# Rests split by time between GpSimd and VectorE, one division for all heads, and no fc1 product of block 1 among the heads of block 0

## The reference

```python
# block 0: int8-like activations, ternary weights, 16 heads of 32 columns
xn = rmsnorm(x, g1) * (1 + scale) + shift
q, k, v = split_heads(bitlinear(xn, w_qkv, b_qkv))
attn = softmax(q @ k.T * 32 ** -0.5)            # per head
o = merge_heads(attn @ v)
x = x + bitlinear(o, w_proj, b_proj)            # act_quant takes max |o| of each row
xn = rmsnorm(x, g2) * (1 + scale2) + shift2
x = x + bitlinear(gelu(bitlinear(xn, w_fc1, b_fc1)), w_fc2, b_fc2)
# block 1: float32, one head of 512 columns
h = film(rmsnorm(x))
x = x + softmax(Q(h) @ K(h).T * 512 ** -0.5) @ V(h) @ proj_w + proj_b
h = film2(rmsnorm(x))
return x + gelu(h @ mlp_w1 + mlp_b1) @ mlp_w2 + mlp_b2
```

## Time and profile before

| | us |
|---|---|
| median of 3 runs | 2530.7 |
| lowest and highest run | 2521.5 and 2537.11 |
| the profiled execution, its time | 2516.55 |
| its span, first to last instruction | 2514.7 |
| mean granted TensorE clock, share of full | 0.923 |
| ScalarE busy, share of the span | 1225.0, 49% |
| GpSimd busy, share of the span | 768.5, 31% |

### The profile page before, as it was taken

How to read it: one execution, slowest core, us unless ns; L and a number is a source line. 1 busy time by engine, 2 the same in 40 slices (tenths; PEclk the granted TensorE clock), 3 DMA queues, 4 the chain that set the end, 5 groups by cost and what they waited for, 6 DMA issues and landing times.

```text
span 2514.7 us, 40181 instructions
## 1 busy us (share of the span) xinstructions
PE 2120.9 (84%) x13525; PEld 1069.9 (43%) x13525; DVE 1683.9 (67%) x2870; ACT 1225.0 (49%) x2032; POOL 768.5 (31%) x684
## 2 busy tenths in 40 slices
PE   4667688878997799779997899789988898789989
PEld 3424344444444444344444444344444344444434
DVE  4578645877578666877578756967587757866422
ACT  6535334474436554464446544564447444574330
POOL 0135101353125422353125412343136312452112
PEclk8777888989999899989999899989999899999989
DMA  7554111302230122202230213102231213101202
GB/s 276 192 181 164 59 51 34 94 18 76 78 113 22 52 75 96 83 18 76 85 105 22 76 51 121 58 29 82 85 97 31 71 60 124 34 35 51 101 23 95
DMA packets 85507, 200.82 MB, mean 80 GB/s; under 512 B 7604, under 2 KB 48856, under 8 KB 73120
## 3 DMA queue, kind: packets, MB, share of 16 engines
q1 hardware_dynamic: 77512, 174.91, 20.6%
q10 hardware_dynamic: 7776, 23.07, 2.6%
HBM read 161.97 MB, written 35.72 MB: 79 GB/s over the span
## 4 chain that ended last, share of the span: by engine, by line
PE 55%; DVE 17%; issue 13%; ACT 10%; POOL 2%; DMA 2%; ACTq 1%; DVEq 0%; SPq 0%; POOLq 0%
PE banks L1213 10%; PE banks L1214 10%; PE banks L1215 10%; PE banks L1170 5%; PE banks L1105 5%; DVE memory L997 4%; PE banks L1061 4%; DVE memory L1046 2%; ACT memory L1042 2%; DVE memory L814 2%; PE banks L991 2%; PE banks L900 1%; ACT L1042 1%; ACT memory L847 1%; PE banks L1035 1%
## 5 line engine op out<-in xcount | busy, mean ns | idle before, releaser
L1213 PE MATMUL banks<-memory 128*128 128x512 bf16 x1536 | 599.8, 390 | 46.9 <-DVE memory L1463 26.6
L1214 PE MATMUL banks<-memory 128*128 128x512 bf16 x1536 | 597.3, 389 | 0.0
L1215 PE MATMUL banks<-memory 128*128 128x512 bf16 x1536 | 595.3, 388 | 0.0
L1046 POOL TENSOR_TENSOR memory<-memory 128x512 bf16<-128x512 f32 x320 | 356.3, 1125 | 499.2 <-ACT memory L1042 497.4
L1042 ACT ACTIVATE memory<-banks 128x512 f32<-128x512 f32 x512 | 283.9, 597 | 216.7 <-PE banks L1035 179.8
L997 DVE TENSOR_REDUCE memory<-banks 128x1 f32<-128x512 f32 x512 | 330.2, 679 | 52.0 <-PE banks L991 51.0
L1441 POOL TENSOR_TENSOR memory<-memory 128x512 bf16<-128x512 f32 x128 | 163.2, 1275 | 512.5 <-DVE memory L1436 512.5
L991 PE MATMUL banks<-memory 96*128 96x512 bf16 x512 | 197.2, 415 | 103.8 <-DVE memory L997 94.4
L1213 PEld LDWEIGHTS banks<-memory 128*128 128x128 bf16 x1536 | 153.6, 100 | 242.0 <-DVE memory L1463 35.0
L1061 PE MATMUL banks<-memory 128*128 128x66 bf16 x4096 | 177.7, 209 | 76.6 <-DVE memory L1046 67.0
L1215 PEld LDWEIGHTS banks<-memory 128*128 128x128 bf16 x1536 | 153.6, 100 | 192.3 <-issue 19.2
(11 more groups left out here) (169 smaller groups left out, 3115.9 us busy)
## 6 DMA issues: line engine op xcount, KB each, us to landing
memory<-weight_parts SPq DMA_DIRECT2D x80, 1024.0 KB, 4.9
memory<-head_parts SPq DMA_DIRECT2D x192, 128.0 KB, 2.7
head_parts<-memory SPq DMA_DIRECT2D x64, 256.0 KB, 2.2
weight_parts<-memory ACTq DMA_DIRECT2D x10, 1024.0 KB, 5.0
memory<-in_L_cond_w_fc SPq DMA_DIRECT2D x2, 4096.0 KB, 14.3
memory<-in_x SPq DMA_DIRECT2D x32, 256.0 KB, 3.2
memory<-ada_rows SPq DMA_DIRECT2D x16, 512.0 KB, 4.6
memory<-in_L_cond_mlp_w ACTq DMA_DIRECT2D x8, 1024.0 KB, 8.8
```

Of the source, the lines that this page charges most:

```text
L1046: eng.tensor_tensor(prob_lo[:, e % RING], expo[:, e % RING], prob_hi[:, e % RING], ALU.subtract).then_inc(ok.sem, 1)
L1213: pe.matmul(bank, lh, rh, start=(k == 0), stop=False)
L1214: pe.matmul(bank, lh, rl, start=False, stop=False)
L1215: mm = pe.matmul(bank, ll, rh, start=False, stop=(k == KC - 1))
```

## The change

- `prob_low`: exponentials 0 to 40 have their rest taken on GpSimd, 41 to 63 on VectorE (FIRST_DVE).
- A head is no longer divided by itself. ScalarE copies its high result out of bank 4 into y (`copy_head`, one slot after the weighing, COPY_AT), VectorE takes the reciprocal of the sums and adds the low result in place. After the last head VectorE divides all of y in four instructions (`divide0`), one for each row tile, before the row maxima.
- M_AT is empty: all products of M come after the slots. Products 0 and 1 stand between head 14 and head 15 on TensorE.
- The tables move: heads are weighed with lags (6, 7, 7, 7) in place of (8, 6, 6, 7); the film turns go from (2, 4) to (2, 10) to (2, 7) to (2, 13); maxima and late q/k parts move by one to three slots.
- GpSimd's four x1 biases follow products 0 to 3 instead of 6 to 9.

```diff
-LATE_HIGH = {(0, 5): ("q", 2), (0, 9): ("k", 2), (1, 4): ("q", 3), (1, 8): ("k", 3)}
-LATE_LOW = {(0, 7): ("q", 2), (0, 11): ("k", 2), (1, 5): ("q", 3), (1, 9): ("k", 3)}
-VALUE_LAG, READ_LAG = ((8, 6, 6, 7), 1)
+LATE_HIGH = {(0, 5): ('q', 2), (0, 9): ('k', 2), (1, 4): ('q', 3), (1, 9): ('k', 3)}
+LATE_LOW = {(0, 6): ('q', 2), (0, 12): ('k', 2), (1, 5): ('q', 3), (1, 9): ('k', 3)}
+VALUE_LAG, COPY_LAG, READ_LAG = ((6, 7, 7, 7), 1, 1)
+FIRST_DVE = 41
+COPY_AT = {later(at, COPY_LAG): h for at, h in VALUES_AT.items()}
-M_AT = ((3, 0), (3, 4), (3, 8), (3, 12), (4, 0), (4, 6))
+M_AT = ()
-TURN_AT = ((2, 4), (2, 6), (2, 8), (2, 10))
+TURN_AT = ((2, 7), (2, 9), (2, 11), (2, 13))
-MAX_AT = {(0, 19): 0, **{(c, 10): c for c in range(1, KC)}}
+MAX_AT = {(0, 19): 0, (1, 8): 1, (2, 10): 2, (3, 10): 3}
-LOW_DVE = [e for e in range(KC * HEADS) if (e % 4 == 3 if e < 3 * HEADS else e % 4 != 0)]
+LOW_DVE = [e for e in range(KC * HEADS) if e >= FIRST_DVE]
...
+        def head_parts(h):
+            o = banks[:, 4, 0:TT * 2 * LOW].rearrange("p (t s n) -> p t s n", t=TT, s=2)
+            return o[:, :, 0, 0:HD], o[:, :, 1, 0:HD], o[:, :, 0, HD], y[:, :, h * HD:(h + 1) * HD]
+        def copy_head(act, i, h):
+            ready(act, plan0, ("o", h), i)
+            high, _, _, out = head_parts(h)
+            act.activation(out, high, ACT.Copy).then_inc(o_copied.sem, 1)
         def read_head(dve, i, h):
             b = ready(dve, plan0, ("o", h), i)
-            dve.reciprocal(sum_inv[:, h % 2], o[:, :, 0, HD]).then_inc(o_small.sem, 1)
...
-            dve.tensor_tensor(o_parts, o[:, :, :, 0:HD], r, ALU.mult).then_inc(free[b].sem, 1)
-            done(dve, plan0, ("o", h), i)
-            dve.tensor_tensor(y[:, :, h * HD:(h + 1) * HD], o_parts[:, :, 0], o_parts[:, :, 1], ALU.add
-                              ).then_inc(o_ok.sem, 1)
+            _, low, total, out = head_parts(h)
+            dve.wait_ge(o_copied.sem, o_copied(i, h + 1))
+            dve.reciprocal(sum_inv[:, :, h], total).then_inc(o_small.sem, 1)
+            dve.tensor_tensor(out, low, out, ALU.add).then_inc(free[b].sem, 1)
+        def divide0(dve, i):
+            done(dve, plan0, ("o", H - 1), i)
+            dve.wait_ge(o_small.sem, o_small(i, H))
+            for t in range(TT):
+                r = sum_inv[:, t].unsqueeze(2).to_broadcast([P, H, HD])
+                dve.tensor_tensor(by_head(y[:, t]), by_head(y[:, t]), r, ALU.mult).then_inc(o_ok.sem, 1)
...
                 for n, job in enumerate(M):
-                    if n >= M_IN:
-                        lows1(j, [job])
-                    if j is not None and M_IN <= n < M_IN + TT:
-                        residual_bias1(pool, j, 1, n - M_IN)
+                    lows1(j, [job])
+                    if j is not None and n < TT:
+                        residual_bias1(pool, j, 1, n)
...
+                if i is not None:
+                    for (c, _), h in COPY_AT.items():
+                        if c > KC:
+                            copy_head(act, i, h)
```

## The result

| | before | after |
|---|---|---|
| median, us | 2533.9 (4 runs) | 2392.84 (4 runs) |
| lowest and highest | 2521.5 and 2542.21 | 2389.83 and 2395.39 |
| the profiled execution | 2516.55 | 2395.26 |

The ratio is 0.9447, with a 95% interval from 0.9403 to 0.949. Ratios compare fast runs alone: beside the kernel without table loads and the one with everything that helped, two of seven runs of before were slow (2538.69 and 2544.43 us).

A forecast was written before the change was run, and what follows sets the result against it. It took VectorE to bound the first half of the heads and ScalarE the second. Seven items at -6.8 us (-48) and item 0 at -7 summed to -55, giving 2476 us by the median, range 2415 to 2530.

The forecast's parts named there:

- Table loads: ScalarE among the heads: 12 function table loads per item, 15.4 us, become one pair.
- Rival D: Heads without the six products: TensorE's clock falls to half rate, +8 us per item, 2582 us; chance 0.10.
- c=2 ... I take 22.5: Second of four rounds of 16 slots in the heads: 22.5 us after the change, bounds 17 and 30.
- the factor 1.35: Round c=2 of the heads: it took 1.35 times VectorE's work, which applied to 17.4 us gives 23.5.
- c=4 to its last score ... 12.5: Last round of the heads: VectorE's 16 rests and 4 heads, 12.9 us, the last few after that score: 12.5.
- proj to fc1 ... as before, at no cost: Between proj and fc1: products 8 to 13 stand as before, at no cost.
- shifts of the turns, ... I cost at nothing: Rounds c=2 and c=3: moving turns, late q/k parts and maxima one to three slots costs nothing.
- It would wait for the same head anyway: ScalarE's 16 head copies, 0.3 us each: it waits for that head anyway, as the next exponential's scores stand behind it.
- that nothing in the passes' first stretch changes: Start of each pass, before the heads' round c=1: the forecast's sum had no term for it.
- rival B: Heads fall to their floor of 63 us, rear 28: -15.8 us per item, 2413 us; chance 0.15.
- the base of 106.8: Heads and rear per item before the change, taken as the mean over items 1 to 7: 106.8 us.
- second road: Heads estimated again from item 0's 70.7 us without splits, plus block 1's 5, less savings: 61 to 69 us.

The follow-up runs named there:

- the kernel without table loads: Kernel before, with the gelu of its six early fc1 products replaced by an Identity with the same bias: 2488.03 us, ratio 0.989.
- the one with everything that helped: Changed kernel plus gelus and casts 0 and 1 ahead of head 15, heads read two places after their copy, sixteen memsets before the loop: 2345.05 us.
- the products alone: Kernel before with one edit, M_AT empty, so all fc1 products of block 1 stand after the heads: 2460.3 us, ratio 0.973.
- shifted: Changed kernel with sixteen tiny memsets ahead of VectorE's preparation, outside the loop: 2368.6 us, ratio 0.937.

## Why the prediction was wrong in size

**Right in direction and in these steps.** *Rests*: 717 ns against my 680, and splitting them by time was worth 68 us alone, at 685 ns. *Copy and add*: 274 and 256 ns against 0.3 and 0.33. *The wait before product 2*: 2.37 us against 2.3. *Table loads*: 8 of L1441 in place of the 50 of L1430 and 42 of L1042. *c=3*: 15.1 against 15.5; *c=1*: 19.5 against 18.5, inside its bounds; *item 0*: 5.6 against 7. *Rival D* did not come: the clock rose, 0.923 to 0.942. Its first half was there, though: with the products alone c=3 and c=4 ran at 0.83 and 0.80. With the whole change both are at 0.94.

**Failed: "c=2 ... I take 22.5".** It took 18.8. I had carried over the factor 1.35 by which that round exceeded VectorE's work. The factor held product 0 of M, which has nothing to do with that work: its slot is (3, 0), but it stands ahead of the key score at which I cut. TensorE before, item 3, its first and last matmul and what follows:
```profile
1083.03 0.64 PE L1213 MATMUL banks<-memory 128*128 128x512 bf16 x1
...
1087.22 0.38 PE L1215 MATMUL banks<-memory 128*128 128x512 bf16 x1
1087.44 0.38 PE L991 MATMUL banks<-memory 96*128 96x512 bf16 x1
```
That is 4.4 of the window's 32.5 us, most of it at half clock, and it left with M_AT. Without it the factor is 1.17 and my own 17.4 us give 20.4. The products alone took 4.0 us off c=2, and putting them back into the change adds 4.7. The change has 19.40 us over 16.39 of VectorE, 1.18, so the rest of the factor held, and my 17.4 was 1.0 too much. With the old tables it is 1.49 (22.6 over 15.2, means), so it is no constant either.

The rest of the factor comes from VectorE's queue. Its timeline before, ahead of the 2.83 us wait of the earlier trace rows: two divisions (L1069 to L1078) and a film rest (L1287) stand between the maxima (L997) that release the scores, and where GpSimd works beside them L1078 takes 1.1 us and L1287 1.44.
```profile
1063.20 0.18 DVE L1069 RECIPROCAL memory<-banks 128x4 f32<-128x4 f32 x1 [0.70 <-PE banks L1061]
1063.48 0.42 DVE L1076 TENSOR_TENSOR memory<-banks,memory 128x256 f32<-128x256 f32 x1
1063.94 1.12 DVE L1078 TENSOR_TENSOR memory<-memory 128x128 f32<-128x128 f32 x1
1064.98 1.28 DVE L997 TENSOR_REDUCE memory<-banks 128x1 f32<-128x512 f32 x2
1066.18 1.44 DVE L1287 TENSOR_TENSOR memory<-memory 128x512 bf16<-128x512 f32 x1
1067.54 0.17 DVE L1069 RECIPROCAL memory<-banks 128x4 f32<-128x4 f32 x1
1067.81 0.42 DVE L1076 TENSOR_TENSOR memory<-banks,memory 128x256 f32<-128x256 f32 x1
1068.27 1.10 DVE L1078 TENSOR_TENSOR memory<-memory 128x128 f32<-128x128 f32 x1
1069.30 1.27 DVE L997 TENSOR_REDUCE memory<-banks 128x1 f32<-128x512 f32 x2
```
The half clock followed the wait; the row has one start after the wait only, in the trace the next stand 0.43 us apart. Per item TensorE now stands 3.6 us in this round where it stood 6.8, at most 1.7 at a time where it was 2.8, and the clock is 0.94 in item 3. GpSimd is busy in all 19.40 us of it, but it is not shown to be what holds the round: with the old rests c=2 took 19.6 at 14.6 us of GpSimd. The Trainium skill (TensorE: Matmul & The Clock Gate, "What's actually happening") has the array at half rate unless kept busy; the trace agrees, 0.94 with about half of the waits gone.

**Failed: "c=4 to its last score ... 12.5".** It took 8.6. I priced the round at VectorE's work, as if its rests had to be done by the last score. The ring of eight lets scores and exponentials run ahead: VectorE was busy 8.07 us in the window where I had 12.9; in item 3 five rests and the reading of head 14 ran behind the last score, beside head 14 and products 0 and 1, which the rear holds anyway. The rear took 28.4, not 31: in item 3 head 14 to the end of head 15 took 8.3 us where I had 11, at full clock (1.13 us for a head, not 1.94).

**Failed: "proj to fc1 ... as before, at no cost".** It gave 4.0 us, with the products alone already. Four gains of block 0 (L814, SBUF to SBUF) took 6.38 us in item 2 before, with three of GpSimd's x1 biases beside them, and the four (L816) take 3.34 after, where the biases come earlier: 3.0 of the 4.0. I had looked at where the biases go and not at what they leave.
VectorE and GpSimd before:
```profile
869.35 6.38 DVE L814 SCALAR_TENSOR_TENSOR memory<-memory 128x512 f32<-128x512 f32 x4
...
870.12 5.06 POOL L1255 TENSOR_TENSOR memory<-memory 128x512 f32<-128x512 f32 x3
```
VectorE after:
```profile
820.01 3.34 DVE L816 SCALAR_TENSOR_TENSOR memory<-memory 128x512 f32<-128x512 f32 x4
```

**Failed: "shifts of the turns, ... I cost at nothing", and the lags, which have no term at all.** The shifts named there were rightly small (6 us for the turns). The lags came into the sum only as one more head of VectorE in c=1, 0.5 us; they are worth 59 of the tables' 62 us. That holds with the new division; with the old one, which has no copy, all tables together are worth 4. I looked whether engines had time for the moved work and not at who stands in line behind whom. The first lag of 8 fills the ring exactly, so ScalarE's next exponential waits for the weighing. Each copy then stands in ScalarE's queue, and VectorE, which waits for it in order, holds maxima, which hold the query scores. "It would wait for the same head anyway" was true of ScalarE (its waits for scores and heads are 215 us before and 214 after) and said nothing of VectorE: 144.4 us with the old tables, at +9 us in the run.

**Failed: that nothing in the passes' first stretch changes.** It cost 4.6 us per item, which no view of before shows: 3.1 at the loop's return, and 1.5 in c=0, whose cause stays open.

By span, the 121 us are, added over the seven passes: heads and rear 112.6, proj to fc1 27.0, item 0 and the ends 11.0, less 29.4 at the passes' starts. The other 20 of the 141 are the distance of the two profiled executions from their medians, which no stretch explains. The errors on the heads, rear and fc1 all lay on one side, and the range was built from cases that shared them: rival B had 63 for the heads and 28 for the rear, where 62.0 and 28.4 came, and I gave it 0.15 on "c=2 never came near its load". That B's 2413 comes nearer to the result is luck in part, since it had nothing for proj to fc1 or for the starts of the passes.

Two slips in the working change nothing: the base of 106.8 is the mean over items 1 to 6 (over 1 to 7 it is 106.7), and the second road's savings of 5.9 and 8.7 are 6.4 and 9.3 by the terms above it.

## What to carry to other kernels

A round that is longer than the work of its busiest engine is not simply scaled by that factor once the engine is unloaded: first take out of the window what will leave it, then ask which waits make the rest. When a job is handed to another engine, look who stands behind it in *both* queues, price the lags too, and retune them with it: the division moved alone lost 9 us, with its lags it won 23. After a change to a looped kernel, compare the first microseconds after the loop's return; a gap without a cause there may go with a shift of the program.

## What the chip showed that I had not expected

*Where a program lies costs time.* In all kernels with the new division VectorE stood 0.4 to 2.2 us (mostly over 1.0) at the start of items 2 to 7 and never at item 1, which is entered without a jump back; in the others, and in the two with sixteen more instructions ahead of the loop, never. Both of those also moved fewer instruction packets on one queue; the page's row of it (packets, MB, share) after:
```profile
q14 instruction: 92, 0.75, 0.1%
```
and shifted:
```profile
q14 instruction: 86, 0.70, 0.1%
```
That is six fewer, and there are six returns. The Trainium skill (Runtime: NRT & Kernel Launch, "Instruction fetch mechanics") says that a taken branch whose target isn't in the current two pages of instructions has to fetch it before it can go on. The place of the stall and these packets agree; but the kernel before and every other one with the old division have 92 too and no stall, so that the fetch is the cause is argued, not shown. Shown, by two kernels, is that instructions ahead of the loop, which do no work in it, take the stall away; that they do so by where they push the loop is the plain reading.

*Waits multiply.* Products and rests give 72 and 68 us alone and some 110 together, the lags 59 and the division from -35 to +23. The tables give 62 or 4, by which division stands beside them. None of the five has a price of its own.
